# Whole-row unpack of packed planes, and a new order of sums and catch-up, in a streamed two-layer graph kernel

## What is computed

```python
def layer0(X, adj, W, b):
    deg = clip(sum(adj, axis=1) + 1, 1)
    z = concat([X, (adj @ X + X) / deg]) @ W + b
    out = relu(z)
    return out / max(norm(out), 1e-12)

def layer1(h, adj, W):
    deg = sum(adj, axis=1)
    return concat([h, adj @ h / (deg + 1)]) @ W.T

x = layernorm(x + layer0(x, adj, W0, b0))
x = layernorm(x + layer1(x, adj, W1))
```

## Time and profile before

| what | value |
|---|---|
| median of three runs | 756.05 us |
| the profiled execution | 757.87 us |
| its span, first to last instruction | 756.1 us |
| TensorE busy, share of the span | 636.0 us, 84% |
| VectorE | 683.7 us, 90% |
| ScalarE | 597.5 us, 79% |
| GpSimd | 310.6 us, 41% |
| HBM read | 270.6 MB, mean 361 GB/s with writes |
| mean granted TensorE clock | 0.939 |

### The profile page before, as it was taken

The page is one execution under the profiler, slowest core; times in us unless marked ns, Lnnn a source line. Parts: engine busy times, 40 slices in busy tenths (PEclk is TensorE's granted clock), DMA queues, the critical chain, the costliest instruction groups (busy, mean ns, idle before and its releaser), DMA issues.

```text
span 756.1 us, 27851 instructions
## 1 busy us (share of the span) xinstructions
PE 636.0 (84%) x11125; PEld 579.3 (77%) x11125; DVE 683.7 (90%) x2517; ACT 597.5 (79%) x905; POOL 310.6 (41%) x344
## 2 busy tenths in 40 slices
PE   1477777667688887888899998999999999999995
PEld 0466766566677776777888898989898998989995
DVE  6877888899999999999989999999999999987994
ACT  6788898888988888889779898888898888860043
POOL 0122524331432346644556565555453535341034
PEclk9976778999999999899989999999999999999999
DMA  9999999999999999999999999999999999910002
GB/s 343 420 421 419 420 419 420 419 420 419 420 419 417 400 421 413 414 391 370 405 355 420 420 418 416 418 418 401 417 404 419 390 422 402 420 68 3 2 26 95
DMA packets 41516, 274.55 MB, mean 363 GB/s; under 512 B 4454, under 2 KB 8614, under 8 KB 8614
## 3 DMA queue, kind: packets, MB, share of 16 engines
q1 hardware_dynamic: 41152, 272.65, 88.4%
q10 hardware_dynamic: 230, 0.07, 0.0%
HBM read 270.60 MB, written 2.10 MB: 361 GB/s over the span
## 4 chain that ended last, share of the span: by engine, by line
PE 37%; DVE 24%; DMA 16%; issue 11%; ACT 6%; POOL 4%; SPq 1%; ACTq 0%; DVEq 0%; POOLq 0%
PE s_ps L387 17%; DMA a_in<-in_adj 16%; DVE e L791 8%; DVE t_sb L798 6%; PE u_ps L406 6%; ACT junk L590 4%; POOL small L1163 3%; PE p_ps L373 2%; PE z_ps L456 2%; DVE u_sb L798 2%; DVE q_sb L860 2%; DVE y_sb L854 2%; PE s_ps L472 2%; PE u_ps L468 1%; PE p_ps L468 1%
## 5 line engine op out<-in xcount | busy, mean ns | idle before, releaser
L590 ACT ACTIVATE junk<-a_in 128x2048 uint8<-128x2048 uint16 x256 | 488.4, 1912 | 18.2 <-DMA a_in<-in_adj 17.6
L387 PE MATMUL s_ps<-xh,t_sb 128*128 128x129 f16 x4096 | 392.2, 253 | 40.6 <-DVE t_sb L798 37.3
L387 PEld LDWEIGHTS s_ps<-xh,t_sb 128*128 128x128 fp8e4 x4096 | 315.1, 103 | 72.1 <-DVE t_sb L798 42.1
L791 DVE TENSOR_SCALAR e<-a_in 128x2048 uint8<-128x2048 f32 x256 | 313.8, 1233 | 26.4 <-DMA a_in<-in_adj 25.5
L1190 POOL COPY store<-pk 128x32 uint32<-128x32 uint32 (+1 forms) x250 | 205.1, 863 | 237.2 <-ACT pk L599 237.2
L798 DVE TENSOR_SCALAR t_sb<-pk 128x128 uint32<-128x128 uint32 x1024 | 153.0, 221 | 4.3 <-ACT pk L599 3.5
L373 PE MATMUL p_ps<-pow_h,e 128*128 128x16 f16 x2048 | 91.1, 171 | 70.4 <-DVE e L791 67.9
L373 PEld LDWEIGHTS p_ps<-pow_h,e 128*128 128x128 f16 x2048 | 77.2, 99 | 88.1 <-DVE e L791 75.9
L1163 POOL TENSOR_TENSOR small<-small,minus_half 128x4 f32<-128x4 f32 x32 | 68.4, 2137 | 161.1 <-DVE small L848 114.6
L406 PE MATMUL u_ps<-xh,u_sb 128*128 128x64 f16 x2976 | 105.2, 192 | 0.0
L406 PEld LDWEIGHTS u_ps<-xh,u_sb 128*128 128x128 fp8e4 x2976 | 100.0, 97 | 1.2
(11 more groups left out here) (119 smaller groups left out, 479.2 us busy)
## 6 DMA issues: line engine op xcount, KB each, us to landing
a_in<-in_adj SPq DMA_DIRECT2D x256, 1024.0 KB, 10.1
xl<-in_x SPq DMA_DIRECT2D x4, 512.0 KB, 12.5
out_h<-e SPq DMA_DIRECT2D x8, 256.0 KB, 2.3
b_sb<-in_L_gnn_b ACTq DMA_DIRECT2D x3, 0.2 KB
w_sb<-in_L_gnn_W ACTq DMA_DIRECT2D x1, 32.0 KB
w_raw<-in_L_gnn_W ACTq DMA_DIRECT2D x1, 32.0 KB
```

Source lines behind the costliest of these rows:

```text
L387: last = nc.tensor.matmul(s_ps[:, n % 2, at:GW], t_sb[:, b // 2, b % 2::2], xh[:, b, at:GW], start=(b == 0), stop=False)
L590: nc.scalar.activation(junk[:, t % 2, :], halves[t % R], ACT.Copy, scale=1.0 / 128, accum_out=half_sum[:, n, c:c + 1]).then_inc(s_half, 1)
L791: nc.vector.tensor_scalar(e8[:, c, :], a_in[:, t % R, :], 1.0, float(CODE), ALU.is_equal, ALU.add).then_inc(s_e, 1)
```

## The change

Packed bytes of a whole row block go out of PSUM in one copy of 512 columns, and a whole row block is unpacked by eight instructions on 256 words, where there were two copies and sixteen instructions on 128 words. `p_ps` is used by row block (n % 2), not by half. The order in a turn becomes:

- VectorE: compare 0, [normalise], compare 1, unpack(n-1), [norm], compare 2, add_piece(n), unpack_piece(n+1), [mean], compare 3, [residual, or low_part and begin_acc].
- ScalarE: sum 0, take_packed(n-1), [take_z], sum 1, take_sums(n-2), [take_h], sum 2, [take_g], sum 3, [take_cat].
- TensorE: [dense], pack 0, catch-up first part, [transpose_h], pack 1, catch-up second part, quarters 0 and 1 of n-1, [dense_h], pack 2, quarter 2, pack 3, [transpose_cat], quarter 3.

The guard on x moves to turns 4, 5, 8 and 9.

```diff
-GUARD = [20, 24, 28, 32]
+GUARD = [4, 5, 8, 9]
...
             def pack_chunk(n, c):
                 pe.wait_ge(s_e, n * NC + c + 1)
-                if c % 2 == 0 and n:
-                    pe.wait_ge(s_pk, (n - 1) * 2 + c // 2 + 1)
+                if c == 0 and n >= 2:
+                    pe.wait_ge(s_pk, n - 1)
                 for u in range(CB // 2):
-                    at = ((c % 2) * CB // 2 + u) * PK
-                    last = nc.tensor.matmul(p_ps[:, c // 2, at:at + PK], e_pair[:, c, u // 2, :, u % 2],
+                    at = (c * CB // 2 + u) * PK
+                    last = nc.tensor.matmul(p_ps[:, n % 2, at:at + PK], e_pair[:, c, u // 2, :, u % 2],
...
             def sum_quarter(n, i):
-                if i % 2 == 0:
-                    pe.wait_ge(s_t, n * 2 + i // 2 + 1)
+                if i == 0:
+                    pe.wait_ge(s_t, n + 1)
...
-                if i % 2:
                     last.then_inc(s_sum, 1)
...
-                for c in range(NC):
-                    pack_chunk(n, c)
-                    if e >= 0 and (k, c) == (1, 3):
-                        transpose_cat(e)
...
-                    sum_quarter(n - 1, c)
-                    if e >= 0 and (k, c) == (3, 0):
-                        transpose_h(e)
-                    if n >= START[1] and c in (1, 2):
-                        catch_up(n, c - 1)
-                    if e >= 0 and (k, c) == (3, 1):
-                        dense_h(e)
+                pack_chunk(n, 0)
+                if n >= START[1]:
+                    catch_up(n, 0)
+                if e >= 0 and k == 3:
+                    transpose_h(e)
+                pack_chunk(n, 1)
+                if n >= START[1]:
+                    catch_up(n, 1)
...
+                sum_quarter(n - 1, 0)
+                sum_quarter(n - 1, 1)
+                if e >= 0 and k == 3:
+                    dense_h(e)
+                pack_chunk(n, 2)
+                sum_quarter(n - 1, 2)
+                pack_chunk(n, 3)
+                if e >= 0 and k == 1:
+                    transpose_cat(e)
+                sum_quarter(n - 1, 3)
...
-            def take_packed(n, h):
-                act.wait_ge(s_pps, n * NC + 2 * h + 2)
+            def take_packed(n):
+                act.wait_ge(s_pps, (n + 1) * NC)
                 if n >= 2:
-                    act.wait_ge(s_t, (n - 2) * 2 + h + 1)
+                    act.wait_ge(s_t, n - 1)
                     act.wait_ge(s_store, n - 1)
-                nc.scalar.activation(pk_u[:, n % 2, h * 256:(h + 1) * 256], p_ps[:, h, 0:256], ACT.Copy,
+                nc.scalar.activation(pk_u[:, n % 2, :], p_ps[:, n % 2, :], ACT.Copy,
...
                 sum_codes(n, 0)
+                if n:
+                    take_packed(n - 1)
                 if e >= 0 and k == 2:
                     take_z(e)
                 sum_codes(n, 1)
-                if n:
-                    take_packed(n - 1, 1)
...
                 sum_codes(n, 2)
-                take_packed(n, 0)
...
-            def unpack(n, h):
-                dve.wait_ge(s_pk, n * 2 + h + 1)
+            def unpack(n):
+                dve.wait_ge(s_pk, n + 1)
                 if n:
-                    dve.wait_ge(s_sum, (n - 1) * 2 + h + 1)
-                half = slice(h * NB // 4, (h + 1) * NB // 4)
-                dst = words(t_sb[:, half, :])
+                    dve.wait_ge(s_sum, n)
+                dst = words(t_sb[:, :, :])
...
                 compare(n, 0)
-                if n:
-                    unpack(n - 1, 0)
                 if e >= 0 and k == 3:
                     normalise(e)
-                if n > START[1]:
-                    add_piece(n - 1)
                 compare(n, 1)
...
-                if n >= START[1]:
-                    unpack_piece(n)
+                if n:
+                    unpack(n - 1)
                 if e >= 0 and k == 2:
                     norm(e)
                 compare(n, 2)
-                if n:
-                    unpack(n - 1, 1)
+                if n >= START[1]:
+                    add_piece(n)
+                if START[1] <= n + 1 < NB:
+                    unpack_piece(n + 1)
                 if e >= 0 and k == 1:
                     mean(e)
                 compare(n, 3)
...
-            unpack(NB - 1, 0)
-            add_piece(NB - 1)
-            unpack(NB - 1, 1)
+            unpack(NB - 1)
```

More of the change, by code:

```diff
@@ L531, in _ @@
                     dense(e)
-                for c in range(NC):
-                    pack_chunk(n, c)
-                    if e >= 0 and (k, c) == (1, 3):
-                        transpose_cat(e)
-                    if n == START[seg(n)] and n and c == 0:
-                        pe.wait_ge(s_glo, low(seg(n)) // BR)
-                    sum_quarter(n - 1, c)
-                    if e >= 0 and (k, c) == (3, 0):
-                        transpose_h(e)
-                    if n >= START[1] and c in (1, 2):
-                        catch_up(n, c - 1)
-                    if e >= 0 and (k, c) == (3, 1):
-                        dense_h(e)
+                pack_chunk(n, 0)
[6 more added lines that the diff above has]
+                    catch_up(n, 1)
+                if n == START[seg(n)]:
+                    pe.wait_ge(s_glo, low(seg(n)) // BR)
+                sum_quarter(n - 1, 0)
[8 more added lines that the diff above has]
+                sum_quarter(n - 1, 3)
             e = NE - 1
@@ L710, in _ @@
             e = NE - 1
-            take_packed(NB - 1, 1)
+            take_packed(NB - 1)
             take_sums(NB - 2)
@@ L799, in unpack_planes @@
                 return ins
-            def unpack(n, h):
-                dve.wait_ge(s_pk, n * 2 + h + 1)
+            def unpack(n):
+                dve.wait_ge(s_pk, n + 1)
                 if n:
-                    dve.wait_ge(s_sum, (n - 1) * 2 + h + 1)
-                half = slice(h * NB // 4, (h + 1) * NB // 4)
-                dst = words(t_sb[:, half, :])
+                    dve.wait_ge(s_sum, n)
+                dst = words(t_sb[:, :, :])
                 unpack_planes(lambda g: dst[:, :, g * 2 * PKW:(g + 1) * 2 * PKW],
-                              pk_w[:, n % 2, :].rearrange("p (u w) -> p u w", w=2 * PKW)[:, half, :]).then_inc(s_t, 1)
+                              pk_w[:, n % 2, :].rearrange("p (u w) -> p u w", w=2 * PKW)).then_inc(s_t, 1)
             def unpack_piece(n):
@@ L1185, in keep @@
             def keep(n):
[L1187 removed]
+                pool.wait_ge(s_pk, n + 1)
                 for s in range(row_seg(n), NQ):
```

3 lines of the change are left out of this document (1 added, 2 removed).

## The result

The changed kernel takes 788.63 us (median of six runs, 786.39 to 791.91) against 755.86 before on the same chip (755.25 to 757.96): a ratio of 1.0431, 95% interval 1.0412 to 1.0450. The forecast was 771. The profiled execution took 789.68 us with a span of 787.8, where that of before took 757.87; the loss to be explained there is 31.8 us.

The account below looks back on a forecast made before the run. From turn 13 the engines' waits, not the stream, bound the kernel: twelve epochs 510.6 us against 498.74 (+11.9), last turns +1.9, tail +1.4, so profiled 757.87 becomes 773.1, median 771. Range 755 to 791.

Parts of the forecast that it names:

- five links: Waits round one epoch, from `transpose_cat` through four unpacks to the next: 3.66, 12.53, 11.17, 8.4 and 8.1 us late, sum 43.9.
- link 4: Unpack of k = 0 to that of k = 1: 8.4 us late, ScalarE's four sums and copies, TensorE's way the same.
- The wider unpack: VectorE's eight instructions on 256 words: about 0.6 us less a turn, some 38 us over 64.
- link 2: Unpack of k = 2 to that of k = 3, all on VectorE in order: 12.53 us late.
- Link 1: `transpose_cat` to the unpack of k = 2, through ScalarE's next sum (1.91) and `take_packed`: 3.66 us late.
- links 3: The third, unpack of k = 3 to that of k = 0, with two quarters of 1.79 us each: 11.17 us late.
- hidden by the stream: Epochs before turn 12, without catch-up: 38.2 us by the loop, below the stream's 39.95, so no loss.
- rival B: Waits lower TensorE's clock; a slow quarter at k = 3 each epoch adds 20.9 us: 792; chance 0.08.
- The tail and the last turns: Last three turns lose 1.9 us; in the tail block 63's sums wait for `take_packed` and a whole unpack: +1.4.
- Guard: Moving it takes up to 10 us from VectorE in turns 20 to 32; cost in early turns taken as zero.
- Rival A: Halves not needed, freed engine time decides; needs links under 41.5 us an epoch on average: 740; chance 0.14.
- Rival C: Loss late, gain early: the loop binds only from turn 45, no change, 756; chance 0.08.

Follow-up runs that it names:

- experiment 9: Changed kernel with each row block unpacked by sixteen instructions on 128 words, copies and order kept: 825.42 us, ratio 1.0907 to the kernel before.
- experiments 1: Changed kernel with `take_packed` ahead of ScalarE's first sum: 760.46 us, ratio 1.0060 to the kernel before.
- experiment 2: Changed kernel with `take_packed` and, at k = 2, `take_z` ahead of ScalarE's first sum: 757.73 us, ratio 1.0017 to the kernel before.
- experiment 5: Changed kernel with unread filler matmuls on TensorE, 28 ahead of the first pack at k = 3, 12 ahead of sums in other turns before 44: 783.51 us.
- experiment 7: Changed kernel with the guard on x back in turns 20, 24, 28 and 32: 793.06 us, ratio 1.0499 to the kernel before.
- experiment 6: Changed kernel with more unread matmuls: 28 at the start of k = 3, 16 behind `transpose_h`, 28 or 16 ahead of sums before turn 44: 783.15 us.
- experiment 8: Kernel before with only the guard moved, to turns 4, 5, 8 and 9: 754.38 us, ratio 0.9970.
- experiment 4: Changed kernel with `take_packed` and `take_z` ahead of the first sum, the k = 3 unpack ahead of `normalise`, `transpose_h` behind quarter 0: 750.34 us, ratio 0.9927.

## Why the forecast was right in kind and too small

- **The bound.** Right. The engines' loop sets the epochs, and the five links hold late to 0.3 us each but for link 4 (9.0 for 8.4), where TensorE's way was priced as equal to ScalarE's and is longer: in the epoch of turn 53 the unpack with its signal takes 2.01 us (1.72 priced), and from the end of the last quarter's 16 tiles to the next unpack 0.33 us pass, in which one more matmul runs (L390), that weren't priced.
- **The wider unpack.** Right in size (38 us off VectorE, 37 us of time by experiment 9), and right that none of it shows against the kernel before. Its lower bound, link 2 longer by 0.5, counted one unpack of four: experiment 9 lengthens links 2 to 5 by 1.9 us in the late epoch of turn 53.
- **Link 2.** Right in sum (12.35 for 12.53), in part by luck. Its 4.55 us from `residual` to `normalise` were read across a half's unpack (the earlier trace rows at 582.42, 1.17 us), which the new order takes away from there. Measured are 4.30, of which 0.90 is a wait for GpSimd's second root that the unpack had filled (timeline of the changed kernel, VectorE):

```profile
607.25 0.98 DVE L878 TENSOR_SCALAR h_sb<-y_sb,small 128x64 f32<-128x64 f32 x4 [0.90 <-POOL small L1163]
```

- **Link 1, `take_packed` behind a sum.** Right, and shown by taking it away: 1.89 us for a sum priced at 1.91. What stands behind it (`take_z`, `low_part`, and the stream) wasn't priced, and needn't be for this change; it is what made experiments 1 and 2 come back short.
- **The step that failed: links 3 and 4 in turns 12 to 43, priced with quarters at full clock,** and with them the 38.2 us that were to be "hidden by the stream" before turn 12. The forecast put rival B's slow quarter behind the wait at k = 3 at 0.08, arguing that "late, with 0.85 us idle in 20, the clock stays full". Late it did: B's mechanism isn't there (3.75 us, clock 1.00). In the middle it is, and the kernel before had shown it: the slow quarter of the earlier trace rows stands behind two waits of TensorE (timeline of the kernel before):

```profile
290.85 0.36 PE L373 MATMUL p_ps<-pow_h,e 128*128 128x16 f16 x8 [2.26 <-DVE e L791]
291.94 3.43 PE L387 MATMUL s_ps<-xh,t_sb 128*128 128x257 f16 x16 [0.72 <-DVE t_sb L798]
```

In the middle of the changed kernel TensorE is busy for 15.98 of 20 us where late it is for 19.72, and quarters behind its waits ran at 1.2 GHz. Links 3 and 4 measured 11.3 and 3.6 us above their terms over eight epochs. Where the clock was full, the epochs of turns 25 (after) and 29 (experiment 5), link 3 was 10.43 and 10.87, close to the forecast's terms. Early, the two epochs took 41.4 and 41.7 by their links, over the stream's 39.95, so they weren't hidden: +2.05 (83.10 us together; 81.92 in experiment 7, without the guard, which the forecast took at zero there, and 81.18 in experiment 5, with fillers). The timeline of the changed kernel shows in turn 8 (TensorE) the same picture: behind a wait of 2.28 us for the unpack the first two quarters of 129 columns take 3.65 us at a granted clock of 0.50 and the third 1.89, where the last takes 1.07.

```profile
100.99 3.65 PE L387 MATMUL s_ps<-xh,t_sb 128*128 128x129 f16 x32 [2.28 <-DVE t_sb L803]
...
104.69 1.89 PE L387 MATMUL s_ps<-xh,t_sb 128*128 128x129 f16 x16
...
106.62 1.07 PE L387 MATMUL s_ps<-xh,t_sb 128*128 128x129 f16 x16
```

- **How far the clock is shown.** Of the 11.3 us of link 3, 9.5 are the longer quarters of experiment 6's table. Link 4 lost 3.9 us under either set of fillers (70.8 to 66.9), which is all of its 3.6. In time, experiment 5 gave 7.8 us of the eight epochs back and experiment 6 only 5.2. Which of TensorE's waits lowers the clock isn't shown.
- **The sum.** 773.1 + 13.4 in the middle + 2.05 before it + 1.2 in the four late epochs + 0.1 at the end - 0.2 at the start gives the profiled 789.7.
- **The tail and the last turns.** Right: 3.4 for 3.3.
- **Guard.** The forecast's loops were reckoned without it; experiment 7 prices it in the new order at some 4.4 us (793.06 - 788.63, by medians), less than half of the 10 us of VectorE's time, and experiment 8 at 2.1 in the old one. Moved early, it wasn't free in the old order (the epoch of turn 9 grew by 1.0).
- **The rule.** The Trainium skill, page Perfetto Trace Analysis, section Optimizing Scalar/DVE Operations, says that larger operations can help if the engine is saturated, and that breaking them up may help if Scalar and Vector aren't saturated but leave bubbles on other engines. The prediction gave the second half without its condition. VectorE was near full late (19.20 of 20 us), so by the page's words the first half applied, and it pointed the wrong way: grouping took 38 us off VectorE, and the kernel lost 33. What decided was the order: 788.63 against 750.34 with the same instructions.

Rival A (740) did not come: its condition was links under 41.5. Experiment 4, which brings them to 40.9 on average over the twelve epochs, takes it most of the way, to 750. Rival C fell with the middle epochs, 43.6 us each where it needed 39.95; late it was right. Rival B's 792 lies close to the measured time by another count: it wanted one slow quarter in each of 12.75 epochs, and there were slow pairs in six of the eight middle epochs and none late.

## What to carry to other kernels

Where several engines are nearly full, write down the round of waits through their queues once, link by link, from one epoch's timeline; here that gave 43.9 us for a measured 44.2. Price each TensorE link at both clock levels unless the stretch in question shows the upper one: that a wait is harmless late in a stream, with TensorE full, tells nothing of the middle. And before coarser steps are given up, look at what stands ahead of the signal that they wait for: three moves in the queues (with `transpose_h` moved beside the third), and no work saved, turned 4.3% slower into 0.7% faster. Some 2 of those last 5.4 us are the guard's move, which earned as much in the old order (experiment 8). And follow a cut through all links: in experiment 2 link 2 fell as foreseen, and link 1 took it back.

## What the runs showed of the hardware

A GpSimd copy that costs 0.2 to 0.4 us can last twenty times as long beside VectorE. The kernel before, timeline of GpSimd and VectorE around one `keep` copy:

```profile
555.95 5.78 POOL L1190 COPY store<-pk 128x64 uint32<-128x64 uint32 x1 [6.23 <-ACT pk L599]
...
555.98 1.22 DVE L791 TENSOR_SCALAR e<-a_in 128x2048 uint8<-128x2048 f32 x1
557.11 1.17 DVE L798 TENSOR_SCALAR t_sb<-pk 128x128 uint32<-128x128 uint32 x8
558.20 2.35 DVE L791 TENSOR_SCALAR e<-a_in 128x2048 uint8<-128x2048 f32 x2
560.47 1.17 DVE L798 TENSOR_SCALAR t_sb<-pk 128x128 uint32<-128x128 uint32 x8
561.71 0.42 DVE L829 TENSOR_TENSOR xl<-u_ps,xl 128x256 f32<-128x256 f32 x1
```

The copy ends as VectorE's run of compares and unpacks ends. In the changed kernel VectorE waits more, and the same 250 copies take 77.0 us in all, 350 ns each, where they took 205.1 us, 863 ns each, before. The other way too: an unpack with which a copy starts takes 1.95 us, others 1.70 (the rows at 620.66 and 609.28 above; the copy stands at 620.69). Of the changed kernel's 64 unpacks, 33 overlap an instruction of GpSimd and take 1.69 to 2.01 us; the 31 others take 1.69 to 1.71. The Trainium skill, page SBUF — State Buffer, section Terms, says that the port pair which VectorE and GpSimd share is held by one of them for a whole instruction, and that the loser is blocked. The rows agree with a blocked GpSimd, but they show it kept out over nineteen instructions of VectorE in a row and not over one; no run took the copies away, so the cause is read from the times alone. GpSimd's root shows the same (3.79 us in experiment 2, 2.03 an epoch earlier), at next to no cost there.
